# An AdaLN block with a ternary feed-forward on one core: TensorE's fillings in the opening as 24 products of 64 columns instead of five of 128 to 512 columns

## The chip, the core and the metric

The kernel runs on one core of a Trainium2 chip. The metric is the device time of one execution in microseconds (us), as the median of several runs. The engines are TensorE (PE; its weight loads are PEld), VectorE (DVE), ScalarE (ACT), GpSimd (POOL) and SyncE (SP), which here only issues transfers. They run beside one another and wait for each other through semaphores.

## The reference, cut to what matters

There are 1024 tokens of 256 features (`x` is 32 x 32 x 256, 32 groups of 32 tokens), and one condition row of 256 features for each group.

```python
ada = (timestep_embed @ ada_w + ada_b)[:, None, :]
shift1, scale1, gate1, shift2, scale2, gate2 = jnp.split(ada, 6, axis=-1)
x1 = _ln(x) * (1.0 + scale1) + shift1
qkv = (x1 @ qkv_w + qkv_b).reshape(Bc, Tc, 3, H, DH)      # H = 16, DH = 128
attn = softmax(einsum('bthd,bshd->bhts', q, k) * scale)
x = x + gate1 * (attn_out @ out_w + out_b)
x2 = _ln(x) * (1.0 + scale2) + shift2
x = x + gate2 * (gelu(x2 @ ffn_w1 + ffn_b1) @ ffn_w2 + ffn_b2)
# then a feed-forward with 8-bit activations and ternary weights, added to the first x
h = silu(_linear_bit(x, w1, g1)) * _linear_bit(x, w2, g2)
out = x_first + _linear_bit(h, w3, g3)
```

## The kernel before, in words

The 1024 tokens are four quarters of 256, the 16 heads four groups of four. A unit is one quarter of the tokens with one group of heads: q and k projections (`qk_unit`, one call for each head), v (`v_unit`), scores, softmax, attention, output projection. Sixteen units run one after the other on TensorE; the second eight also carry the two feed-forwards. Each projection is done as three products of fp32r halves (`three_pass`, L580): high by high, low by high, high by low. The order of the work on each engine is written out by hand, as are the semaphore waits. The weights of one group of heads are loaded into `stage` by SyncE and split into `w_hi` and `w_lo` by the other engines.

The change touches the opening, TensorE's program before the first unit (L909 to L934). `probs_t` serves there as `filler`: VectorE sets 128 x 128 of it to one (L1146), TensorE multiplies it by itself into `att_bank[1]`, and nothing reads the result. `keep_wide(n)` (L913) is one f32 product of the filler with n copies of itself, so 128n columns; `keep_running` (L909) is used elsewhere. TensorE's opening is, in its own order:

1. `keep_wide(4)`, `keep_wide(1)`, as soon as the filler is made.
2. Two transposes of the condition rows (L923), which wait for `cond_in`, a load that SyncE issues first of all (L469). ScalarE copies the result to `cond_t` (L1924, behind the load of its table) and raises `cols_made`.
3. `keep_wide(2)`.
4. Four products for the two column blocks of `scale1` (`ada_cols`, L701), which wait for `cols_made` and the weights.
5. The transpose of the bias rows (L929); ScalarE copies it to `bias_cols` (L1926).
6. `x_turn(0)`: four transposes (L725) of the normalised first quarter `xn`. They wait for VectorE's `x_norm` (L1168), which stands behind the load of x (L1766, on ScalarE's queue), the statistics (L1154, L1157, L1159) and GpSimd's power (L2117).
7. Four products for `shift1` (`ada_cols` into `out_bank`).
8. `keep_wide(1)`, `keep_wide(4)`.
9. `opening_qk` (L607): the first head's q and k in f32 straight from `stage` and `x2` (L613), which waits for `x1_ready`; then the second head in three passes.

Beside it, `opening_x` on VectorE (L1206) takes the results of 4 to 7 and makes x1: the scale part (L1197), a product with the turned x (L1212), the shift part (L1199), a sum (L1216), which raises `x1_ready`. It goes on with the low halves of the weights (L1204) and of x1 (L1219). ScalarE makes the high halves (L1801, L1929). SyncE waits for the first projection (L481) before it issues the loads of the second group of heads. The tile named `xt` in the profile is `x2` of the code, `work` and `stage` hold weights, `gate` in the rows of L725 is `xn`.

Of the kernel before, what the change touches and what calls it, by code (L numbers as in the profile page):

```python
# [14 lines left out]
P = 128  # L15
# [52 lines left out]
def adaln_bitffn(nc, x, cond, ada_w, ada_b, qkv_w, qkv_b, out_w, out_b, ffn_w1, ffn_b1, ffn_w2, ffn_b2,  # L68
# [52 lines left out]
    with ExitStack() as ctx:  # L121
# [135 lines left out]
        filler = probs_t[:, 0:P // TB, :].rearrange("p a c -> p (a c)")  # L257
# [4 lines left out]
        proj_bank, att_bank, wide_bank = [[pair[:, i, :] for i in range(2)] for pair in (proj_banks, att_banks, wide_banks)]  # L262
# [305 lines left out]
        def _(pe):  # L568
# [38 lines left out]
            def opening_qk():  # L607
                pe.wait_ge(x1_ready, 1)
                pe.wait_ge(qkw_in[0], 32)
                for s in range(2):  # L610
                    for k in range(KD):
                        c0 = (s * KD + k) * HW
                        mm = pe.matmul(proj_bank[0][:, s * QT:(s + 1) * QT], stage[:, c0:c0 + P], x2[:, k, :],  # L613
                                       start=(k == 0), stop=(k == KD - 1))
                mm.then_inc(projected, 1)
                pe.wait_ge(x1_hi_made, 1)
                pe.wait_ge(qk_hi, 1)
                pe.wait_ge(qk_lo, 1)
                qk_unit(0, 1, ("rhs", (x1_lo_made, 1)))
# [75 lines left out]
            def ada_cols(dst, first, loaded, columns, copies=1, last=True):  # L695
                n = copies * NB
                for j in columns:
                    pe.wait_ge(loaded[j // KD], 16)
                    for k in range(KD):
                        c0 = first + j * P  # L700
                        mm = pe.matmul(dst[:, j * n:(j + 1) * n].rearrange("p (r b) -> p r b", r=copies),  # L701
                                       ada_w_sb[:, k, c0:c0 + P],
                                       cond_t[:, k, :].unsqueeze(1).broadcast_to([P, copies, NB]),
                                       start=(k == 0), stop=(k == KD - 1))
                if last:
                    mm.then_inc(ada_mm, 1)
# [203 lines left out]
                for i in range(n):  # L910
                    pe.matmul(bank[:, 0:P], of, of, start=True, stop=True)

            def keep_wide(n):  # L913
                pe.matmul(att_bank[1][:, 0:n * P].rearrange("p (r c) -> p r c", r=n), filler,
                          filler.unsqueeze(1).broadcast_to([P, n, P]), start=True, stop=True)

            pe.wait_ge(filler_made, 1)
            keep_wide(4)
            keep_wide(1)
            pe.wait_ge(ident_made, 2)  # L920
            pe.wait_ge(cond_in, 16)
            for k in range(KD):
                mm = pe.transpose(proj_bank[0][:, k * NB:(k + 1) * NB], cond_rows[:, k * P:(k + 1) * P], ident[0:NB, 0:NB])  # L923
            mm.then_inc(turned0, 1)
            keep_wide(2)
            pe.wait_ge(cols_made, 1)
            ada_cols(proj_bank[1], 0, ada1_in, (KD, KD + 1), ADA_COPIES)
            pe.wait_ge(bias_in, 48)
            pe.transpose(att_bank[0][:, 0:NBIAS], bias_rows, ident[0:NBIAS, 0:NBIAS]).then_inc(turned0, 1)  # L929
            x_turn(0)  # L930
            ada_cols(out_bank, 0, ada1_in, range(KD), ADA_COPIES)
            keep_wide(1)
            keep_wide(4)
            opening_qk()  # L934


# [1378 lines left out]
```

## Time and profile before

| | |
|---|---|
| median of 3 runs | 319.81 us (319.61 to 320.64) |
| the profiled execution | 318.95 us |
| its span, first to last instruction | 316.8 us |
| granted TensorE clock, mean | 1.00 |
| PE busy | 309.0 us, 98% |
| PEld busy | 274.4 us, 87% |
| DVE busy | 221.2 us, 70% |
| ACT busy | 183.2 us, 58% |
| POOL busy | 127.0 us, 40% |
| DMA | 24.41 MB, mean 77 GB/s |

The profiled execution is one of its own, 0.86 us below the median. The span leaves out 2.15 us around the instructions. Busy times of different engines overlap. TensorE's matmuls are pipelined and their ends are modelled, so one record's length reaches into the next record; where the pace matters, the distance from one start to the next is read. Times in the rows are microseconds from the start of the span.

### The profile page before, as it was taken

The numbers are of one execution on the slowest core, as the hardware profiler recorded it, in microseconds if no ns is written. First come the engines' busy times: TensorE is split into PE (matmuls) and PEld (weight loads), VectorE is DVE, ScalarE is ACT, GpSimd is POOL, SyncE is SP. The second block draws the span as 40 slices with busy tenths as digits, with TensorE's granted clock in tenths as the row PEclk, the third lists the DMA queues.
The fourth block names the chain that finished last, engine by engine and source line by source line (L and its number), as shares of the span: only waits on it lengthen the run. The fifth ranks groups of instructions, "written<-read, shape, count | busy, mean of one in ns | idle before, by whom it ended". The sixth has DMA issues, their size and how long they took to land.

```text
span 316.8 us, 9833 instructions
## 1 busy us (share of the span) xinstructions
PE 309.0 (98%) x4183; PEld 274.4 (87%) x4183; DVE 221.2 (70%) x448; ACT 183.2 (58%) x354; POOL 127.0 (40%) x109
## 2 busy tenths in 40 slices
PE   8999999999999999999999999999999999999986
PEld 5879989899897989888898998879998879998665
DVE  4647888757795994524559048789277698995996
ACT  2747384555534574466344827587455768377793
POOL 2357405200940982666220612247330254215590
PEclk9999999999999999999999999999999999999999
DMA  7991990500049442110020010200010200200001
GB/s 238 332 354 43 294 323 8 168 2 2 2 110 225 140 128 105 54 49 2 3 69 2 2 34 3 67 2 2 23 47 0 68 4 2 68 0 2 0 33 68
DMA packets 21027, 24.41 MB, mean 77 GB/s; under 512 B 1973, under 2 KB 18521, under 8 KB 20985
## 3 DMA queue, kind: packets, MB, share of 16 engines
q1 hardware_dynamic: 20608, 23.50, 24.1%
q8 instruction: 33, 0.54, 0.7%
q10 hardware_dynamic: 376, 0.30, 0.3%
q14 instruction: 10, 0.07, 0.1%
HBM read 22.68 MB, written 1.11 MB: 75 GB/s over the span
## 4 chain that ended last, share of the span: by engine, by line
PE 91%; ACT 4%; DVE 1%; issue 1%; DMA 1%; POOL 0%; ACTq 0%; DVEq 0%; POOLq 0%
PE proj_banks L580 43%; PE out_bank L580 17%; PE wide_banks L580 5%; PE turn_bank L580 4%; PE att_banks L675 3%; PE proj_banks L645 3%; PE wide_banks L867 3%; PE att_banks L580 2%; PE wide_banks L675 1%; ACT work L1913 1%; DMA xin<-in_x 1%; PE att_banks L867 1%; PE wide_banks L750 1%; PE proj_banks L867 1%; ACT L1784 1%
## 5 line engine op out<-in xcount | busy, mean ns | idle before, releaser
L1779 ACT ACTIVATE q_t<-proj_banks,bias_cols 128x256 f32<-128x256 f32 x64 | 30.3, 474 | 47.6 <-PE proj_banks L580 46.7
L580 PE MATMUL proj_banks<-x_hi,w_hi 128*128 128x256 f32 x252 | 53.0, 292 | 0.0
L580 PE MATMUL proj_banks<-x_lo,w_hi 128*128 128x256 f32 x252 | 49.8, 279 | 0.0
L580 PE MATMUL proj_banks<-x_hi,w_lo 128*128 128x256 f32 x252 | 49.8, 279 | 0.0
L580 PEld LDWEIGHTS proj_banks<-x_hi,w_hi 128*128 128x128 f32 x252 | 38.7, 189 | 3.6 <-issue 1.4
L580 PEld LDWEIGHTS proj_banks<-x_lo,w_hi 128*128 128x128 f32 x252 | 38.5, 189 | 0.0
L580 PEld LDWEIGHTS proj_banks<-x_hi,w_lo 128*128 128x128 f32 x252 | 38.3, 188 | 0.0
L1273 DVE TENSOR_TENSOR v_sb<-proj_banks,bv_row 128x512 f32<-128x512 f32 x32 | 22.0, 687 | 16.5 <-PE proj_banks L580 16.0
L1779 ACT ACTIVATE k_t<-proj_banks,bias_cols 128x256 f32<-128x256 f32 x64 | 30.0, 469 | 0.0
L1784 ACT ACTIVATE scores<-scores 128x256 f32<-128x256 f32 x16 | 6.7, 417 | 27.9 <-DVE scores L1282 27.9
L1299 DVE STREAM_TRANSPOSE att_banks<-att_banks 128x512 f32<-128x512 f32 x16 | 11.6, 726 | 15.8 <-PE wide_banks L675 15.3
L580 PE MATMUL out_bank<-wo_hi,at_hi 128*128 128x256 f32 x128 | 21.6, 291 | 0.3
L2126 POOL TENSOR_TENSOR w_lo<-stage,w_hi 128x1024 fp32r<-128x1024 f32 x6 | 14.3, 2387 | 17.6 <-DVE w_hi L1228 13.7
L580 PE MATMUL proj_banks<-w_hi,x_hi 128*128 128x512 f32 x64 | 20.6, 404 | 0.4 <-ACT k_t L1779 0.4
L2185 POOL TENSOR_TENSOR h_lo<-work,h_hi 128x512 fp32r<-128x512 f32 x10 | 13.2, 1322 | 18.2 <-ACT h_hi L1866 17.8
L580 PE MATMUL proj_banks<-w_lo,x_hi 128*128 128x512 f32 x64 | 20.0, 394 | 0.0
L580 PE MATMUL proj_banks<-w_hi,x_lo 128*128 128x512 f32 x64 | 20.0, 394 | 0.0
L580 PE MATMUL out_bank<-wo_hi,at_lo 128*128 128x256 f32 x128 | 19.9, 278 | 0.0
L580 PE MATMUL out_bank<-wo_lo,at_hi 128*128 128x256 f32 x128 | 19.9, 278 | 0.0
L2157 POOL TENSOR_TENSOR xa<-xa,out_b_row 128x512 f32<-128x512 f32 x4 | 7.0, 1750 | 31.9 <-ACT xa L1795 31.9
L580 PEld LDWEIGHTS out_bank<-wo_hi,at_hi 128*128 128x128 f32 x128 | 17.1, 188 | 2.1 <-issue 1.4
L580 PEld LDWEIGHTS out_bank<-wo_lo,at_hi 128*128 128x128 f32 x128 | 17.1, 188 | 0.0
(328 smaller groups left out, 785.8 us busy)
## 6 DMA issues: line engine op xcount, KB each, us to landing
stage<-in_L_cond_qkv_w SPq DMA_DIRECT2D x16, 256.0 KB, 4.4
gate<-gate_rows_scratch SPq DMA_DIRECT2D x48, 64.0 KB, 2.6
stage<-in_L_cond_qkv_w SPq DMA_DIRECT2D x4, 512.0 KB, 5.6
stage<-in_L_cond_out_w SPq DMA_DIRECT2D x16, 128.0 KB, 3.6
work<-in_L_ffn_w SPq DMA_DIRECT2D x2, 1024.0 KB, 9.2
xin<-in_x SPq DMA_DIRECT2D x7, 256.0 KB, 2.8
bv_row<-in_L_cond_qkv_b SPq DMA_DIRECT2D x4, 256.0 KB, 5.5
work<-in_L_cond_ada_w SPq DMA_DIRECT2D x1, 1024.0 KB, 8.8
```

What stands on the lines that cost most here:

```text
L580: mm = pe.matmul(dst, l, r, start=start and i == 0, stop=stop and i == len(seq) - 1)
L645: mm = pe.matmul(packed[j * TB:(j + 1) * TB, cols], q_t[:, h, tok], k_t[:, h, tok], start=True, stop=True)
L675: mm = pe.matmul(dst, probs_t[r, t * HG + h, :], v_sb[r, t, h * P:(h + 1) * P], start=True, stop=True)
L750: mm = pe.transpose(dst[:, m * P:(m + 1) * P], tern[p % 2][:, c0:c0 + P], ident_h[:, :])
L867: mm = pe.matmul(banks[i][:, :], qt_bf[:, b, t, i * KD + k, :], w12t[:, i, k, c * MC:(c + 1) * MC], start=(k == 0), stop=(k == KD - 1))
L1273: dve.tensor_tensor(v_sb[:, t, :], proj_bank[t][:, :], bv_row[:, u % 2, :], ALU.add).then_inc(v_kept, 1)
L1299: dve.transpose(att_from(u, p), attended_rows(u, p)).then_inc(at_turned, 1)
L1779: act.activation(dst[:, h, :], proj_bank[h % 2][:, s * QT:(s + 1) * QT], ACT.Identity, bias=bias_cols[:, c:c + 1]).then_inc(qk_kept, 1)
L1784: act.activation(scores[:, :, :], scores[:, :, :], ACT.Exp, scale=SM_SCALE).then_inc(exp_done, 1)
L2126: pool.tensor_tensor(w_lo[g % 2][:, s], stage[:, s], w_hi[g % 2][:, s].bitcast(F32), ALU.subtract).then_inc(qk_lo, 1)
L2157: pool.tensor_tensor(xa[:, :, :], xa[:, :, :], rows, ALU.add).then_inc(acc_biased, 1)
L2185: pool.tensor_tensor(h_lo[:, m, :], hf(2 * j, 2), h_hi[:, m, :].bitcast(F32), ALU.subtract).then_inc(h_lo_made, 1)
```

## The change

The helper `keep_wide`, which makes one product of n x 128 columns, is replaced by `keep_narrow`, which makes n products of 64 columns each with the same stationary tile of 128 x 128. The calls in the opening become 10, 4 and 10 products. Nothing else is changed.

```diff
-            def keep_wide(n):
-                pe.matmul(att_bank[1][:, 0:n * P].rearrange("p (r c) -> p r c", r=n), filler,
-                          filler.unsqueeze(1).broadcast_to([P, n, P]), start=True, stop=True)
+            def keep_narrow(n):
+                for i in range(n):
+                    pe.matmul(att_bank[1][:, 0:P // 2], filler, filler[:, 0:P // 2], start=True, stop=True)
 
             pe.wait_ge(filler_made, 1)
-            keep_wide(4)
-            keep_wide(1)
+            keep_narrow(10)
             pe.wait_ge(ident_made, 2)
             pe.wait_ge(cond_in, 16)
             for k in range(KD):
                 mm = pe.transpose(proj_bank[0][:, k * NB:(k + 1) * NB], cond_rows[:, k * P:(k + 1) * P], ident[0:NB, 0:NB])
             mm.then_inc(turned0, 1)
-            keep_wide(2)
+            keep_narrow(4)
             pe.wait_ge(cols_made, 1)
             ada_cols(proj_bank[1], 0, ada1_in, (KD, KD + 1), ADA_COPIES)
             pe.wait_ge(bias_in, 48)
             pe.transpose(att_bank[0][:, 0:NBIAS], bias_rows, ident[0:NBIAS, 0:NBIAS]).then_inc(turned0, 1)
             x_turn(0)
             ada_cols(out_bank, 0, ada1_in, range(KD), ADA_COPIES)
-            keep_wide(1)
-            keep_wide(4)
+            keep_narrow(10)
             opening_qk()
```

## Rows read from the trace of the kernel before

**Rows 1.** The page: PE's busy time, granted clock in 40 slices, chain by line.

```profile
PE 309.0 (98%) x4183; PEld 274.4 (87%) x4183; DVE 221.2 (70%) x448; ACT 183.2 (58%) x354; POOL 127.0 (40%) x109
...
PEclk9999999999999999999999999999999999999999
...
PE proj_banks L580 43%; PE out_bank L580 17%; PE wide_banks L580 5%; PE turn_bank L580 4%; PE att_banks L675 3%; PE proj_banks L645 3%; PE wide_banks L867 3%; PE att_banks L580 2%; PE wide_banks L675 1%; ACT work L1913 1%; DMA xin<-in_x 1%; PE att_banks L867 1%; PE wide_banks L750 1%; PE proj_banks L867 1%; ACT L1784 1%
```

**Rows 2.** Busy time by stretch: PE, PEld, DVE, ACT, POOL, clock, DMA share, GB/s.

```profile
9.00:20.00 11.00, 11.00 (x93) 10.13 (x96) 6.08 (x13) 6.81 (x12) 3.07 (x3) 1.00 1.08 333
9.00:80.00 71.00, 71.00 (x1044) 64.38 (x1044) 51.30 (x105) 41.05 (x75) 24.26 (x13) 1.00 0.52 165
300.00:316.80 16.80, 12.27 (x109) 9.67 (x106) 13.64 (x28) 11.51 (x17) 9.20 (x12) 1.00 0.14 48
```

**Rows 3.** The chain that ended last, opening and end: start, length, what.

```profile
0.72 2.78 DMA xin<-in_x
...
306.21 1.14 ACT work L1913 x2
```

**Rows 4.** Timeline of PE in the opening, short stretches: start, length, operation.

```profile
1.04 1.22 PE L914 MATMUL att_banks<-probs_t 128*128 128x512 f32 x1 [1.04 <-DVE probs_t L1146]
...
2.05 1.06 PE L914 MATMUL att_banks<-probs_t 128*128 128x512 f32 x1
...
2.91 0.64 PE L914 MATMUL att_banks<-probs_t 128*128 128x128 f32 x2
...
3.12 0.42 PE L914 MATMUL att_banks<-probs_t 128*128 128x128 f32 x1
...
3.60 0.29 PE L923 MATMUL proj_banks<-ident,scores 32*128 32x32 f32 x1
...
4.83 0.36 PE L701 MATMUL proj_banks<-cond_t,work 128*128 128x128 f32 x1
...
5.03 0.39 PE L701 MATMUL proj_banks<-cond_t,work 128*128 128x128 f32 x2
...
5.81 0.22 PE L929 MATMUL att_banks<-ident,v_sb 68*128 68x68 f32 x1
...
7.84 0.28 PE L914 MATMUL att_banks<-probs_t 128*128 128x128 f32 x1
...
8.06 0.59 PE L914 MATMUL att_banks<-probs_t 128*128 128x512 f32 x1
...
8.50 0.59 PE L914 MATMUL att_banks<-probs_t 128*128 128x512 f32 x1
...
9.05 0.48 PE L613 MATMUL proj_banks<-xt,stage 128*128 128x256 f32 x1
```

**Rows 5.** Timeline of the opening: weight loads, transposes of x, ScalarE, VectorE.

```profile
1.04 0.29 PEld L914 LDWEIGHTS att_banks<-probs_t 128*128 128x128 f32 x1 [1.04 <-DVE probs_t L1146]
...
1.21 0.33 PEld L914 LDWEIGHTS att_banks<-probs_t 128*128 128x128 f32 x1
...
4.06 0.19 ACT L1924 COPY cond_t<-proj_banks 128x64 f32<-128x64 f32 x1
...
6.45 0.66 PE L725 MATMUL turn_bank<-ident,gate 128*128 128x128 f32 x4 [0.42 <-DVE gate L1168]
...
7.73 0.53 PEld L914 LDWEIGHTS att_banks<-probs_t 128*128 128x128 f32 x4
...
8.30 0.69 DVE L1216 TENSOR_TENSOR xt<-xt,ada_t 128x512 f32<-128x512 f32 x1
```

**Rows 6.** Timeline of PE: the records with 32 moving columns, second and last.

```profile
18.06 0.39 PE L701 MATMUL wide_banks<-cond_t,work 128*128 128x32 f32 x2
...
19.62 0.28 PE L701 MATMUL wide_banks<-cond_t,work 128*128 128x32 f32 x1
```

**Rows 7.** Transfers: the condition's load, and ScalarE's wait for group 1's weights.

```profile
scores<-in_cond SPq DMA_DIRECT2D x1, 32.0 KB, 2.0
...
18.87 1.04 ACT L1801 CAST w_hi<-stage 128x1024 fp32r<-128x1024 f32 x1 [2.60 <-DMA stage<-in_L_cond_qkv_w]
```

## The prediction, made before the change was run

> **What bounds the kernel now.** I read the page first. PE is busy for 309.0 of 316.8 us, and the chain that ended last is mostly its own: 43% of the span in the projection products of L580 on proj_banks alone [rows 1]. Busy time by stretch shows where PE has room: none between 9 and 80 us, but 4.5 us behind 300 [rows 2], where the chain runs through ScalarE's squares [rows 3]. That late idle is dependence among stages, not slack waiting for the opening: its producers come later when PE comes later. So what delays the start of the projections moves the end by as much, and the question is what the 24 products do to the opening.
>
> The chain of the first 12 us shows what the opening hangs on [rows 3]: the load of x (landed at 3.50), its statistics on VectorE, a power on GpSimd, the normalisation, then from 6.45 TensorE without a gap: four transposes, eight records of ada products, the last fillings, the first projection at 9.05 [rows 4, 5]. Before 6.45 TensorE is ahead of that chain: its idle of 0.42 us before the transposes, behind the bias transpose of 5.81, is the only slack it has there [rows 4, 5].
>
> One record is not one product. Each f32 product stands as two MATMUL records, each with a weight load (5 fillings make ten of each) [rows 4]. I take paces from starts, as the ends are modelled. The granted clock is printed as full for the whole span [rows 1, 2], yet the starts of the opening show two levels. The second 512-column record starts at 2.05 and the next at 2.91: 0.86 us. At the end of the opening the same record takes 0.44 us, from 8.06 to 8.50 [rows 4]. These are TensorE's 1.2 and 2.4 GHz, at two passes of the columns for each record. The ada record that starts at 4.83 still takes 0.20 us to the next start; the seven from 5.03 to the bias transpose at 5.81 take 0.11 each. So the clock rises at about 5.0; ahead of that TensorE streamed columns from 1.04 on nearly without a break.
>
> **The change part by part.** The streamed columns stay as they are: 4+1 blocks of 128 become 10 x 64, 2 blocks 4 x 64, 1+4 blocks 10 x 64. Weight loads and records grow from 10 to 48. So the price hangs on the weight loads: does a record of 64 columns take what its columns want (2 x 64 at 2.4 GHz, 0.053 us), or what its load wants?
>
> *Pace at the high clock.* The nearest row is L701 into wide_banks: 128-column weights and only 32 moving columns. Its starts run from 18.06 to 19.62 over 14 steps, 0.111 us each [rows 6]. With 128 moving columns the pace is 0.11 too (the seven from 5.03) [rows 4]. A quarter of the columns saves nothing: the load of 128 columns sets the pace, and 64 columns lie between the two. I take 0.111 us.
>
> *Pace at the low clock.* No row shows a run of short products there; it must be bounded. From below: 0.11, if a load doesn't follow the clock. From above: 0.21, the 128-column records of 2.91 to 3.12. The first pair of loads says that they do follow: 0.29 and 0.33 us long at the low clock (starts 1.04 and 1.21, so ends 0.21 apart); at the high one four loads take 0.53 in all, 0.11 from one to the next, which leaves 0.19 for each [rows 5]. I take 0.21 and keep 0.11 as the other end.
> The Trainium skill ("TensorE: Matmul & The Clock Gate", LDWEIGHTS) gives a load as its columns over 1.2 GHz, 107 ns for 128, and names no other value for the lower clock. The high-clock rows agree at 0.111; by that rule the low-clock pace would be 0.107 as well. The rows on the loads' lengths speak against it; its result is the second rival.
>
> *First fillings.* The first 512-column record took 1.01 us against 0.86 for the second, so 0.15 goes to the first load; streaming begins at 1.19. By 5.0 about 18 records of 0.21 are done, the other two take 0.11 each: end near 5.2, where it was 3.12 + 0.21 = 3.33 [rows 4]. The two condition transposes, which had their data by then (cond lands 2.0 us after its issue, the first on its queue [rows 7]), start near 5.2, the second at 5.3 instead of 3.60. At the high clock they take 0.2: 5.4.
> *Middle fillings.* Eight records of 0.111: 0.9, end 6.3. The cover for ScalarE's copy of cond_t holds: the copy was done at 4.25, 0.65 after the second transpose started at 3.60 [rows 4, 5]. New: 5.3 + 0.65 = 5.95, ahead of 6.3.
> *Ada, bias.* Eight ada records and the bias transpose, 1.0: 7.3. Here the slack is gone: the x transposes, ready at 6.41, start at 7.3 instead of 6.45. This is 0.85 on the path. They and the second ada group take 1.39 as before (6.45 to 7.84): 8.7.
> *Last fillings.* 20 x 0.111 = 2.2 instead of 8.94 - 7.84 = 1.10: end 10.9. First projection near 10.95, before 9.05: **+1.9 us**, of which 0.85 from the late transposes and 1.05 from the last ten products.
>
> *What was beside.* VectorE must have x1 ready: its final add ended at 8.99, 1.15 after TensorE had streamed the second ada group (7.84) [rows 4, 5]. With that group streamed at 8.7 it ends at 9.85, a microsecond before TensorE is free, so TensorE's own queue now sets the start. VectorE's split of w and x_lo follow by 0.85, and the second head wants them at 12.9: covered. SP waits for the first projection before it loads group 1; these loads go out 1.9 later. The DMA engines are full until 20 us, and ScalarE's copy of group 1 waited 2.6 us for its data at 18.87 [rows 2, 7], so the backlog hides most of this; if it didn't, the data would be later by the same 1.9 as TensorE, and cost nothing more. No wait is added.
>
> *Sum.* Against the profiled execution: 318.95 + 1.9 = 320.85 (span 318.7). The median of the runs lies 0.86 above the profiled one: 319.81 + 1.9 = **321.7 us**.
>
> **The rivals.**
> *A later rise of the clock* (0.32). Short products leave the array without columns for some half of the time; what stood ahead of the rise at 5.0 was a nearly unbroken stream. If the rise comes later for it, each us of lateness costs half a us on a queue that has no slack. As far end I take a rise as late behind the first ada record as it now is behind the first filling (3.96 us): fillings end at 5.4, transposes 5.75, fillings 7.45, ada from there at 0.21; the rise comes at 11.4; x transposes start at 9.35 and end at 10.2, the rest of ada ends at 11.65, the fillings at 13.85: +4.85. Halfway between this and +1.9 is +3.4: 323.2. For it: half-empty streaming has no row ahead of a rise. Against it: the 32-column run at 18 us keeps its pace of 0.111 [rows 6], though that is behind the rise.
> The Trainium skill (same page, the section on the clock gate) says that the warm-up is a matter of time and not of the number of matmuls. By it the rise would come as before, which is the forecast; no run here shows it yet.
> *Loads don't follow the clock* (0.17). Low-clock pace 0.11: the first two groups of fillings end where they did, the x transposes stay at 6.45, and only the last ten cost, 7.84 + 2.2 = 10.05 against 9.05: +1.05, 320.9. Intermediate paces give +1.05 to +1.9.
> *Not slower* (0.06). All 24 products have the same stationary tile. If a repeated load costs 0.055 or less, the columns set the pace, the same columns take the same time, and the result is 319.8. Rows for a 128-column filling can't exclude it (7.84 to 7.95, 0.11, either way); the 32-column row has a new tile each time. Against: the last two fillings load this tile four times in a row, 0.11 apart [rows 5]. It decides at a pace of 0.06: there the last ten end before x1 is ready. A gain is nearly excluded: x lands no earlier, and the transposes of 6.45 wait for it.
> The remaining 0.45 is the forecast.
>
> **How the numbers follow.** A measurement of this kernel can tell 0.3% (0.96 us) from no change. The forecast and the later clock are slower beyond that; of the second rival half falls on each side. Slower 0.86, same 0.11, faster 0.03 (a luckier moment of the clock's rise or noise). Range: down to the second rival, 320.7; up to a little past the middle of the later clock, 323.7. Below it lies the case of no change, above it the worst of the clock.
>
> **What would show it.** Right: 20 records of 0.111 ahead of L613, which starts near 10.95; x transposes released by PE's own queue near 7.3, their idle of 0.42 gone; starts 0.21 apart before 5; from 12 us on every start later by one constant. Wrong: short records 0.055 apart; records still 0.21 apart behind 5.3; x transposes still at 6.45; or PE idle ahead of group 1's products near 25 us, by which the shift would grow further on.

## The result, and the profile after

The changed kernel took 324.07 us in the median of 5 runs (323.0 to 324.31), the kernel before 319.81 (319.61 to 320.64, 5 runs). The ratio is 1.0122, with an interval of 1.0093 to 1.0151: slower by 4.3 us, where +1.9 was forecast and 323.7 was the upper end of the range.

The page of the changed kernel, its span, PE's busy time and the chain by engine:

```profile
span 320.8 us, 9909 instructions
...
PE 313.8 (98%) x4221; PEld 281.5 (88%) x4221; DVE 221.9 (69%) x448; ACT 183.4 (57%) x354; POOL 127.1 (40%) x109
...
PEclk9999999999999999999999999999999999999999
...
PE 91%; DVE 4%; ACT 4%; issue 1%; DVEq 0%; ACTq 0%
```

PE has 38 records more than in [rows 1], as counted (48 for 10), and 4.8 us more of busy time. VectorE, ScalarE and GpSimd are busy as long as before, within 0.7 us. The granted clock is still printed as full.

The timeline of PE in the opening, merged over 0 to 17 us (start, length, operation), and below it the same engine in short stretches, to be read against [rows 4]:

```profile
1.04 4.53 PE L915 MATMUL att_banks<-probs_t 128*128 128x64 f32 x20 [1.04 <-DVE probs_t L1144]
...
5.50 0.42 PE L922 MATMUL proj_banks<-ident,scores 32*128 32x32 f32 x2
...
5.85 1.97 PE L915 MATMUL att_banks<-probs_t 128*128 128x64 f32 x8
...
7.61 2.02 PE L701 MATMUL proj_banks<-cond_t,work 128*128 128x128 f32 x8
...
9.53 0.70 PE L725 MATMUL turn_bank<-ident,gate 128*128 128x128 f32 x4
...
10.07 1.06 PE L701 MATMUL out_bank<-cond_t,work 128*128 128x128 f32 x8
...
10.97 2.34 PE L915 MATMUL att_banks<-probs_t 128*128 128x64 f32 x20
```

```profile
5.15 0.42 PE L915 MATMUL att_banks<-probs_t 128*128 128x64 f32 x1
5.50 0.31 PE L922 MATMUL proj_banks<-ident,scores 32*128 32x32 f32 x1
...
9.42 0.32 PE L928 MATMUL att_banks<-ident,v_sb 68*128 68x68 f32 x1
9.53 0.37 PE L725 MATMUL turn_bank<-ident,gate 128*128 128x128 f32 x1
...
9.74 0.49 PE L725 MATMUL turn_bank<-ident,gate 128*128 128x128 f32 x3
...
9.85 0.38 PE L725 MATMUL turn_bank<-ident,gate 128*128 128x128 f32 x2
...
13.15 0.43 PE L613 MATMUL proj_banks<-xt,stage 128*128 128x256 f32 x1
```

A group's length tells the clock: eight f32 records of 64 or 128 columns take 2.0 us at the low clock and 1.1 at the high one, twenty of them 4.5 and 2.3, the four transposes 1.06 and 0.66. Here the first 20, the next 8 and the first ada group are all at the low clock. The first ada group, which starts at 4.83 in [rows 4], took 1.14 us before and now takes 2.02. The x transposes hold the rise: the second starts 0.21 after the first, the third 0.11 after the second (9.74, 9.85). So the clock rises near 9.7, not at 5.0. The trace bears this out: its list of granted levels opens with full speed at 9.73 us, at 5.00 in the kernel before, and has nothing ahead of that entry. The first projection starts at 13.15 instead of 9.05: +4.10. The span grew by 4.0, the profiled execution by 4.05 (323.0 against 318.95).

The same stretch on VectorE and ScalarE, to be read against [rows 5], shows that no other engine sets the start:

```profile
5.74 0.74 DVE L1166 TENSOR_SCALAR gate<-xin,mv,rstd 128x256 f32<-128x256 f32 x2 [0.91 <-POOL rstd L2115]
...
9.78 0.22 ACT L1924 COPY bias_cols<-att_banks 128x68 f32<-128x68 f32 x1 [3.61 <-PE att_banks L928]
...
11.42 0.69 DVE L1214 TENSOR_TENSOR xt<-xt,ada_t 128x512 f32<-128x512 f32 x1
```

The normalised x is ready near 6.5 and waits three microseconds for TensorE. VectorE's sum ends at 12.11, one microsecond ahead of the first projection.

### The profile page after: what moved, and what is told of

Its sections match the earlier page's. It is cut to its first block, busy times and chain, and to the rows that moved or that the text cites. A ratio compares the mean times of both kernels' runs of the same rounds, so it can differ in the third digit from the quotient of the medians.

```text
span 320.8 us, 9909 instructions
## 1 busy us (share of the span) xinstructions
PE 313.8 (98%) x4221; PEld 281.5 (88%) x4221; DVE 221.9 (69%) x448; ACT 183.4 (57%) x354; POOL 127.1 (40%) x109
## 4 chain that ended last, share of the span: by engine, by line
PE 91%; DVE 4%; ACT 4%; issue 1%; DVEq 0%; ACTq 0%
PE proj_banks L580 43%; PE out_bank L580 16%; PE wide_banks L580 5%; PE turn_bank L580 4%; PE att_banks L675 3%; PE proj_banks L645 3%; PE att_banks L915 3%; PE wide_banks L867 2%; PE att_banks L580 2%; PE wide_banks L675 1%; ACT work L1911 1%; DVE w_hi L1226 1%; PE att_banks L867 1%; PE turn_bank L725 1%; PE att_banks L901 1%
## 6 DMA issues: line engine op xcount, KB each, us to landing
work<-in_L_cond_ada_w SPq DMA_DIRECT2D x1, 1024.0 KB, 10.5
```

## The experiments

Theory after the result: the extra 4.1 us of the opening are a longer queue on TensorE (its weight loads) plus a later rise of the clock, and the rise is later because columns stream only half of the time. Rivals: the number of instructions or the length of the queue holds the clock down; the moment of the rise is luck; part of the price sits elsewhere. Twelve runs were made in three sets, each set beside the kernel before. Unless said otherwise a diff is against the kernel before; `keep_narrow(n)` makes n products of 64 columns as in the change.

Three words are used below. The head is the first two groups of fillings (10 and 4 products in the change), the tail is the last group, ahead of the first projection. A head is dense when it is made of the old wide products. The first ada group is the four products for `scale1`, the second the four for `shift1`, as in the list of the opening.

What the profiles showed, the moment of the rise read from the starts in short stretches (the start from which the next is 0.11 away). The first full-speed entry in the list of granted levels of each trace lies within 0.25 us of it; for e3_cols128 it is 5.98. The last column has the run's median and that of the kernel before in its set. The tail is dense in e2_head, e7_none and the kernel before with and without the moved load, absent in e9_last_none, and made of narrow products in all others (ten, in e4_half five).

| kernel | head fillings | rise | first projection | span | median, kernel before |
|---|---|---|---|---|---|
| before | dense | 5.0 | 9.05 | 316.8 | 319.81 |
| before again | dense | 6.6 | 9.26 | 318.4 | 320.20, 320.07 |
| e1_tail | dense | 5.0 | 10.23 | 318.2 | 320.67, 320.15 |
| e9_last_none | dense | 6.1 | 9.16 | 317.9 | 319.91, 320.07 |
| e10_ada_early | dense | 5.0 | 9.24 | 317.0 | 319.59, 319.88 |
| e3_cols128 | 14 x 128 | 6.2 | 11.47 | 319.8 | 321.27, 320.15 |
| e5_cols96 | 14 x 96 | 10.5 | 13.57 | 321.3 | 323.23, 319.88 |
| changed kernel | 14 x 64 | 9.7 | 13.15 | 320.8 | 324.07, 319.81 |
| changed, again | 14 x 64 | 10.4 | 13.46 | 320.9 | 323.72, 320.07 |
| e11_after_ada_early | 14 x 64 | 10.1 | 13.29 | 321.1 | 323.63, 319.88 |
| e2_head | 14 x 64 | 11.5 | 13.03 | 320.8 | 322.67, 320.15 |
| e6_cols32 | 14 x 32 | 11.1 | 13.71 | 321.5 | 323.91, 319.88 |
| e4_half | 7 x 64 | 9.6 | 10.41 | 318.7 | 320.79, 320.15 |
| e7_none | none | 8.7 | 10.25 | 318.3 | 320.49, 320.07 |

**e3_cols128: is it the columns?** The changed kernel with 128 instead of 64 columns in each of the 24 products.

```diff
-            def keep_narrow(n):
...
+            def keep_narrow(n, c=128):
...
-                    pe.matmul(att_bank[1][:, 0:P // 2], filler, filler[:, 0:P // 2], start=True, stop=True)
+                    pe.matmul(att_bank[1][:, 0:c], filler, filler[:, 0:c], start=True, stop=True)
```

> The same 24 products with the same loads, but of 128 columns each, so that the array is given columns all the time while every record still takes what its load takes (0.21 us at the low clock, 0.11 at the high one). Theory (the clock rises late because half of the time no columns stream): the rise comes back to near 5.0, the rest is the longer queue alone, first projection near 10.95, 321.7. Rival (the many short instructions or the longer queue hold the clock down, whatever the columns): rise near 9.5 and 324.1, as with 64 columns.

321.27 us, ratio 1.0026 (1.0007 to 1.0045). The timeline of PE, merged:

```profile
1.04 4.63 PE L919 MATMUL att_banks<-probs_t 128*128 128x128 f32 x20 [1.04 <-DVE probs_t L1148]
5.60 0.42 PE L926 MATMUL proj_banks<-ident,scores 32*128 32x32 f32 x2
5.95 1.16 PE L919 MATMUL att_banks<-probs_t 128*128 128x128 f32 x8
6.94 1.06 PE L701 MATMUL proj_banks<-cond_t,work 128*128 128x128 f32 x8
```

The same number of instructions, the same loads, starts that agree within 0.1 us up to the middle fillings, and twice the columns: these fillings take 1.16 instead of 1.97 us and the clock is up from 6.2 (5.98 by the trace's list). Neither the number of instructions nor the length of the queue holds it down. Nor is it the luck of one profile: the twelve times of this kernel lie at 320.71 to 322.45, the eleven of the changed kernel at 323.0 to 325.05. What is left, the longer queue and a rise at 6.0, costs 2.4 us at the first projection and 1.1 in the median. From here to the changed kernel's 13.15 are 1.7 us more, for a rise 3.75 us later (9.73 against 5.98): close to half a us for each us.

**e4_half: the length of the queue taken away.** Five, two and five products of 64 columns, so that the queue is as long as before.

```diff
-            keep_wide(4)
-            keep_wide(1)
+            keep_narrow(5)
...
-            keep_wide(2)
+            keep_narrow(2)
...
-            keep_wide(1)
-            keep_wide(4)
+            keep_narrow(5)
```

> Half of the 64-column products (5, 2 and 5), so that TensorE's queue is as long as before at either clock: 10 records of 0.21 end at 3.4, 4 more at 4.7, 10 of 0.11 at the end take 1.1. Theory (half-empty streaming delays the rise): the rise is still late, near 9; the first ada group takes 1.7 instead of 0.9, x transposes start near 6.8, the second ada group ends near 9.2 and the first projection starts near 10.3: +1.3, 321.1. Rival (only the length of the queue counts): rise near 5.0, 319.8.

320.79 us, ratio 1.0017 (1.0002 to 1.0033), span 318.7. PE, merged:

```profile
3.37 0.42 PE L926 MATMUL proj_banks<-ident,scores 32*128 32x32 f32 x2
3.71 1.11 PE L919 MATMUL att_banks<-probs_t 128*128 128x64 f32 x4
4.62 2.02 PE L701 MATMUL proj_banks<-cond_t,work 128*128 128x128 f32 x8
...
6.55 1.06 PE L725 MATMUL turn_bank<-ident,gate 128*128 128x128 f32 x4
7.40 1.92 PE L701 MATMUL out_bank<-cond_t,work 128*128 128x128 f32 x8
```

TensorE is at the condition transposes as early as before (3.37), and yet both ada groups run at the low clock; the first projection starts at 10.41, as expected (10.3). The median rose by only 0.6 us where 1.3 was expected; e10_ada_early and e11_after_ada_early below are about that.

**e5_cols96 and e6_cols32: by degrees, or one of two?** The changed kernel with 96 and with 32 columns (`c=96` and `c=32` in the diff of e3_cols128).

> The 24 products with 96 columns each: same loads and same starts, columns for three quarters of the time instead of half. Theory (the more columns stream, the earlier the rise, by degrees): rise between 6.2 and 9.5, first projection 11.5 to 13, 321.3 to 323.0. Rival (it is one or the other: like 128 columns, or like 64): rise near 6 and 321.2, or behind 9.7 and 323.7.

> The 24 products with 32 columns each: same loads and same starts, columns for a quarter of the time. Theory (by degrees): rise later than with 64 columns, 11 to 13, first projection 13.8 to 14.8, 324.2 to 325.2. Rival (below some share products count the same): rise at 9.7 to 11.5 as with 64, first projection 13.1 to 14.1, 323.7.

With 96 columns 323.23 us (1.0098, 1.0064 to 1.0132), with 32 columns 323.91 (1.0134, 1.0113 to 1.0156). The two profiles, PE's first ada group, x transposes and second ada group:

```profile
7.71 1.97 PE L701 MATMUL proj_banks<-cond_t,work 128*128 128x128 f32 x8
...
9.59 1.05 PE L725 MATMUL turn_bank<-ident,gate 128*128 128x128 f32 x4
10.44 1.09 PE L701 MATMUL out_bank<-cond_t,work 128*128 128x128 f32 x8
```

```profile
7.52 2.05 PE L701 MATMUL proj_banks<-cond_t,work 128*128 128x128 f32 x8
...
9.48 1.06 PE L725 MATMUL turn_bank<-ident,gate 128*128 128x128 f32 x4
10.33 1.39 PE L701 MATMUL out_bank<-cond_t,work 128*128 128x128 f32 x8
```

Both rise within the spread of the four profiles with a 64-column head (9.7 to 11.5). The expectation by degrees failed for 96 columns (a rise by 9.5, at most 323.0), and for 32 columns the time and the first projection are those of its rival, while 11.1 fits either. One profile of each was taken. Two of the six times with 96 columns were 321.08 and 321.13, near the 321.27 of 128 columns, the others 322.99 to 324.32. That 96 columns now and then bring the early rise would fit, but no profile caught it; it stays open. No run separates the columns of one product from the share of the time in which columns stream, since the loads keep the pace the same.

**e1_tail and e2_head: which group costs what.** Short products in the last group alone, and in the first two alone.

```diff
             ada_cols(out_bank, 0, ada1_in, range(KD), ADA_COPIES)
-            keep_wide(1)
-            keep_wide(4)
+            keep_narrow(10)
             opening_qk()
```

> Only the last five-block filling is made of ten 64-column products; the first two groups are as before. Theory (one 64-column record takes 0.11 us at the high clock, and the clock's late rise comes from the short products at the head alone): TensorE is free 1.05 us later, the first projection starts near 10.1 instead of 9.05, the clock rises near 5.0 as before; 319.8 + 1.05 = 320.9. Rival (the last group is hidden behind VectorE's x1, all of the 4.3 us comes from the head): 319.8, first projection at 9.05.

```diff
-            keep_wide(4)
-            keep_wide(1)
+            keep_narrow(10)
...
-            keep_wide(2)
+            keep_narrow(4)
```

> The first two groups are 64-column products, the last is as before. Theory: low-clock starts 0.21 apart up to a rise near 9.5 as in the changed kernel, the last fillings take 1.1 us; the first projection now waits for VectorE's sum at 12.1 and starts near 12.15: +3.1, 322.9 to 323.1. Rival (the rise is as before, the extra time is a longer queue only): +0.85, 320.7.

The tail alone: 320.67 us, 1.0018 (0.9995 to 1.0041), rise at 5.0, first projection at 10.23. Its queue is longer by the expected 1.05. The rest is a later start of the x transposes (6.67 instead of 6.45): the bias transpose had waited for its rows (0.5 us of idle), and the normalised x, too, was ready only at 6.6 in this profile. The head alone: 322.67 us, 1.0074 (1.0049 to 1.0098), first projection at 13.03. The PE timeline of e2_head, merged, and VectorE's sum:

```profile
9.54 1.06 PE L725 MATMUL turn_bank<-ident,gate 128*128 128x128 f32 x4
10.39 1.60 PE L701 MATMUL out_bank<-cond_t,work 128*128 128x128 f32 x8
11.82 1.25 PE L914 MATMUL att_banks<-probs_t 128*128 128x128 f32 x4
13.03 0.48 PE L613 MATMUL proj_banks<-xt,stage 128*128 128x256 f32 x1
...
12.28 0.69 DVE L1219 TENSOR_TENSOR xt<-xt,ada_t 128x512 f32<-128x512 f32 x1
```

The rise came at 11.5 here, in the middle of the second ada group, although the head is that of the changed kernel. As expected VectorE's sum sets the start; it ends at 12.97 and not at 12.1, because most of the second ada group ran at the low clock. The medians say 0.5 for the tail and 2.5 for the head; their sum of 3.0 is under the 3.65 to 4.3 of the whole change, but not by more than the intervals leave open.

**after_again and before_again: how far the moment of the rise moves.** The two kernels once more, unchanged.

> The changed kernel once more, beside the runs of this call, so that its time and the moment of its rise can be compared with them. Theory: low-clock starts 0.21 apart until a rise somewhere between 9.5 and 11.5, first projection 13.1 to 14.1, 1.0 to 1.4% above the kernel before. Rival (the first result was due to the chip or the moment, the rise can also come near 5): +1.9, 0.6%.

> The kernel before once more, for a second profile: whether its rise always comes near 5.0. Theory: it comes between 5 and 6.5, first projection at 9.05 to 9.5, time as before. Rival: the moment of the rise is a matter of luck whatever the products are, and can lie behind 9 here too; then the first projection is at 10.5 or later and the time 321.5 or more.

The changed kernel: 323.72 us, 1.0100 (1.0070 to 1.0131), rise at 10.4. The kernel before: 320.20, 0.9995 (0.9972 to 1.0018), rise at 6.6, a tenth beyond what was expected. In its profile the first ada group is at the low clock too. A second thing shows at 19.35, at the later ada products of 32 columns [rows 6]: TensorE waits for SP's second load of ada weights.

```profile
4.83 1.98 PE L701 MATMUL proj_banks<-cond_t,work 128*128 128x128 f32 x8
6.63 0.25 PE L929 MATMUL att_banks<-ident,v_sb 68*128 68x68 f32 x1
6.71 0.61 PE L725 MATMUL turn_bank<-ident,gate 128*128 128x128 f32 x4
...
9.26 0.48 PE L613 MATMUL proj_banks<-xt,stage 128*128 128x256 f32 x1
...
19.35 1.97 PE L701 MATMUL wide_banks<-cond_t,work 128*128 128x32 f32 x16 [0.91 <-DMA work<-in_L_cond_ada_w]
```

A rise 1.6 us later costs it 0.2 us at the first projection: TensorE's late ada group is just done when x is ready. The moment of the rise moves by 1.6 to 1.8 us among profiles with the same head, but in no profile is it later than 6.6 with a dense head or earlier than 9.6 with a short one.

**e7_none and e9_last_none: what fillings are worth.** No fillings ahead of the first ada group; and none ahead of the first projection.

```diff
-            keep_wide(4)
-            keep_wide(1)
...
-            keep_wide(2)
```

> No fillings at all ahead of the first ada group; the last group as before. TensorE is then empty up to the condition transposes near 3.2, waits for ScalarE's copy until 4.4, and streams ada records of 128 columns from there. Theory (only streamed columns bring the rise, short products next to nothing): rise between 7 and 9.5, x transposes at 6.5, first projection between 9.9 and 10.7, +0.9 to +1.7, 320.7 to 321.5, that is faster than the changed kernel by over 2. Rival (the short products at the head bring the rise nearer, though late): without them it comes later than in the changed kernel, behind 10, first projection at 11 or later, 322 or more.

```diff
-            keep_wide(1)
-            keep_wide(4)
             opening_qk()
```

> Head as before, no fillings ahead of the first projection. Theory: they only bridge TensorE's wait for VectorE's x1, from 7.95 to 9.0; the clock stays up over that gap; first projection at 9.05, 319.8 to 320.1, no difference from before. Rival: the gap of 1.1 us brings the clock down, starts of the projection's records 0.43 apart instead of 0.21, +2 or more.

Without the head: 320.49 us, 1.0004 (0.9986 to 1.0022), a little under the expected 320.7; without the last group: 319.91, 1.0007 (0.9977 to 1.0036). Neither can be told from the kernel before, so neither group of fillings is shown to earn anything here. PE of e7_none, merged:

```profile
2.91 0.39 PE L925 MATMUL proj_banks<-ident,scores 32*128 32x32 f32 x2 [2.91 <-DMA scores<-in_cond]
4.61 2.05 PE L701 MATMUL proj_banks<-cond_t,work 128*128 128x128 f32 x8 [1.31 <-DMA work<-in_L_cond_ada_w]
...
7.64 1.57 PE L701 MATMUL out_bank<-cond_t,work 128*128 128x128 f32 x8
9.05 1.25 PE L914 MATMUL att_banks<-probs_t 128*128 128x128 f32 x4
```

The rise comes at 8.7, with full records from 4.61 on. An empty head is 2.2 us better than a short one with the same wide tail (320.49 against 322.67 in e2_head, the kernels before beside them at 320.07 and 320.15). The short head holds back the full records of the first ada group, from 4.61 to 7.61, and the rise came later with it. It isn't nothing for the clock, though: the rise came 2.1 to 3.9 us behind the first of these records in the four profiles with a 64-column head, 4.1 us with an empty one. That the late work is what made the rise late is argued from these distances and not shown by a run of its own.

PE of e9_last_none:

```profile
9.16 0.48 PE L613 MATMUL proj_banks<-xt,stage 128*128 128x256 f32 x1 [1.04 <-DVE xt L1218]
```

Without the last group TensorE is idle for 1.04 us ahead of the projection, and the clock stays up: the projection's starts are 0.22 apart behind the first, as in the kernel before. Four of its twelve times lay at 321.05 to 323.68, though; whether the clock falls in some executions wasn't seen.

**e10_ada_early and e11_after_ada_early: where part of the shift goes.** SP's second load of ada weights moved ahead of the loads of wo, in the kernel before and in the changed one.

```diff
             load_x(1, x_in[1])
-            load_wo(0)
             load_bv(0)
             sp.dma_start(ada_w_sb[:, :, 2 * D:6 * D], adaw_d[:, :, 2 * D:6 * D]).then_inc(ada2_in, 16)
+            load_wo(0)
```

> The kernel before, only that SP issues the second load of ada weights (L478) ahead of the four loads of wo instead of behind them. In two of the profiles TensorE waits 0.4 to 0.9 us for it at the second ada group near 18.6 to 19.3. Theory (this wait is what hides part of a later opening, and what costs the kernel before some time in most of its runs): the wait is gone, that group starts right behind the projections, near 18.1 to 18.4, and the median is 0.4 to 0.9 lower: 319.2 to 319.7. Rival (the wait is rare, or the loads moved behind it are waited for in its place): no difference, 320.1, or a wait of ScalarE for wo.

> The changed kernel with the same move of the load. Theory: here TensorE is too late to wait for it, so nothing changes: 323.7, and the distance to the kernel before with the same move is the full shift of the first projection, 4.0 to 4.6, larger than the 3.65 between the unmoved ones. Rival (what hides part of the shift is somewhere else): the distance stays at 3.6.

319.59 us, 0.9997 (0.9977 to 1.0017), and 323.63, 1.0121 (1.0101 to 1.0142). The later ada products of 32 columns in either profile, e10_ada_early and then e11_after_ada_early:

```profile
18.14 1.87 PE L701 MATMUL wide_banks<-cond_t,work 128*128 128x32 f32 x16
```

```profile
22.15 1.87 PE L701 MATMUL wide_banks<-cond_t,work 128*128 128x32 f32 x16
```

The profile of e10_ada_early has no wait for this load. Of the profiles with the load in its old place and a dense head, before_again has one of 0.91 us and e9_last_none one of 0.41, the first profile of the kernel before and e1_tail have none. The distance of the two medians, 4.04 us, is that of their first projections (13.29 - 9.24 = 4.05), where the unmoved kernels of the second set were 3.65 apart for 4.20. That would fit the theory that this load hides part of a later opening. But the difference of 0.4 is smaller than the intervals, and the gain of 0.4 to 0.9 us that was expected of e10_ada_early didn't show. So what hides part of the shift stays open.

## Why the prediction was wrong

**The step that failed** is the one of the first fillings: "By 5.0 about 18 records of 0.21 are done, the other two take 0.11 each". It carried the moment of the rise over from the kernel before into a kernel in which short products ran ahead of it. All of 20 + 8 + 8 records ran at 0.21 instead, and the clock rose at 9.7. Put this in place of 5.0, and the prediction's own price of half a us for each us gives 1.9 + 4.7 / 2 = 4.25, against 4.10 measured at the first projection and 4.3 in the medians.

**The rival that came true** is the later rise. Its far end (+4.85, rise at 11.4) was nearer than its middle (+3.4): the profiles gave rises at 9.7, 10.4, 10.1 and 11.5. That is partly luck, as the far end took a rise 3.96 us behind the first ada record, where the four profiles show 2.1 to 3.9. The rival had 0.32, and what lay above 323.7 of it, about its upper third, was cut off by the range. That was too low, because its price was a midpoint between two ends and the rows had nothing that spoke for the middle; and what was held against it, the 32-column run at 18 us, tells only that a high clock stays up [rows 6]. The Trainium skill ("TensorE: Matmul & The Clock Gate", the section on the clock gate) says that the warm-up is a matter of time and not of the number of matmuls. Of the number the traces agree: the same 24 products with 128 columns rise at 6.2. Of the time they don't, as I read it, as if any steady issue would do: the profiles with 96, 64 and 32 columns show the rise 3.5 to 5.3 us later at the same times of issue, and the measurement decides.

**What held.** The high-clock pace of a 64-column record: 20 from 10.97 to 13.15, 2.18 us for 2.2. The low-clock pace: 0.21 (5.15 is the last of 20 starts, 4.11 us behind the first, 0.216 each, first load included). With 32, 96 and 128 columns it is 0.21 as well. So the pace that doesn't depend on the columns, which I take for that of the loads, does follow the clock, and the second rival is out. The Trainium skill (same page, LDWEIGHTS) gives a load of 128 columns as 107 ns by its formula, with no other value for the lower clock; this fits the high-clock rows alone. That the queue and not VectorE sets the start: 1.04 us between them, one microsecond forecast. The queue's price, +1.9 at the first projection: e3_cols128 paid 2.4, of which some 0.5 is its rise at 6.0 instead of 5.0, at half a us for each us.

**What may be partly wrong** is that nothing behind 9 us absorbs. The profiled pair carried 4.10 as 4.0, but there the kernel before had its ada weights in time; in before_again it waited 0.91 us for them. The medians of e1_tail, e3_cols128 and e4_half rose by 0.5, 1.1 and 0.6 us for first projections later by 1.2, 2.4 and 1.4 than 9.05. The wait for the weights could be why; that it is isn't shown, and one profile can lie on either side of a median (e3_cols128 ran 321.93 us when profiled, 0.66 above its own). One profile of the kernel before was too few to see that wait.

## What to carry to other kernels

Many short f32 products aren't a cheaper way to fill TensorE: each record takes what its load of 128 columns takes (0.11 us at the high clock, 0.21 at the low one), and in these runs the clock rose at 9.6 to 11.5 us behind a head of 32 to 96 columns and at 5.0 to 6.6 behind one of 128 to 512. Whatever stands ahead of the clock's rise is to be priced with the rise moved, the late case written out to its end and given its full share of the range. And fillings that outlast what they bridge can be worse than none (2.2 us here), since they hold back the real work behind them.

## What was not expected of the hardware

- At the same instructions and loads, and at starts within 0.1 us, 128 columns for each product brought the rise at 6.2, 96 columns at 10.5, 64 at 9.7 to 11.5, 32 at 11.1: in these few profiles one of two outcomes, not a slope.
- The moment of the rise differs between executions of one program: 5.0 and 6.6 for the kernel before, 9.7 and 10.4 for the changed one.
- The mean granted clock was printed as 0.999 or 1.00 although the first 5 to 11 us ran at 1.2 GHz by the starts. The trace's list of levels has no entry ahead of the rise, and the mean counts that stretch as full; the 0.999 of the changed kernel is a fall in its last 0.5 us. In an opening the distances between starts are the thing to read.
